# Products of zeros on TensorE in the later half of a first layer's head, and at its end

## The chip, the cores and the metric

One core of one Trainium2 chip runs the whole program. The metric is the device time of one execution in microseconds (us), from start to end; the kernel is launched once and computes everything.

## The reference

Two transformer layers on x of shape (2, 1024, 256) in float32. Layer 0 is causal attention with 16 heads of width 16 in 4 groups (each group shares its key and value head), with unit-length queries and keys, rotary tables, and then a feed-forward product on block-quantised operands. Layer 1 is causal attention with 16 heads and a mixture of eight experts. A layer norm follows each. Only the beginning of layer 0 matters here:

```python
q = (x @ Wq + bq)...; k = (x @ Wk + bk)...; v = (x @ Wv + bv)...
q_hat = q / (norm(q) + EPS); k_hat = k / (norm(k) + EPS)
q_r = apply_rope(q_hat * alpha * sqrt(hd)); k_r = apply_rope(k_hat)
scores = einsum(q_r, k_r) / sqrt(hd)    # causal, softmax, times v
```

## The kernel before

The program is written by hand: each engine has one list of instructions, run in order, and semaphores tie the lists together. PE is TensorE, DVE is VectorE, ACT is ScalarE, POOL is GpSimd, SP is the engine that issues the transfers.

The **head** (`head()`) makes the queries and keys of layer 0. Its work is cut into 12 units (`NU`), u = 0 to 11: four chunks m of 512 tokens by three tiles n of 128 rows (two of queries, one of keys). A unit goes through these steps, each on its engine:

- PE `projected(u)` (L649), four recorded pieces of a product in float32 into bank A.
- PE `begin(u)` (L667): one product of zeros, one row by 128 weights by 512 columns in bfloat16, that opens bank R + u % 2, after a wait for `s_sq`, that is until ACT has read what stood there two units before.
- DVE `turned(u)` (L799, two instructions), after `begin(u)`. One goes straight into the opened bank.
- PE `rotate(u)` (L673, two pieces), which adds the rotated half to that bank.
- ACT `keep(u)` (L750 copy, L754 square), the square goes on to PE `lengths(u)` (L684: 8 pieces of 4 or 8 columns, into bank N = 7).
- Once three units of a chunk have their lengths, DVE `factors(m, 0)` and `factors(m, 1)` (L838 to L855, some twenty small instructions on 80 columns) work out the inverse lengths, PE `factors(m)` turns them (L697), ACT copies them (L771).
- PE `spread_factors(u)` (L707, 60 rows by 512 columns), DVE `normalised(u)` (L808), ACT `keep_hi(u)` (L758), DVE `less_hi(u)` (L815), ACT `keep_mid(u)` (L762), POOL (L787): the unit is cut into three bfloat16 parts in `parts_mem`. POOL counts them in `s_parts`.

PE's list runs over u = 0 to 20 (`NU + LATER + 2` with `LATER` = 7): in round u it does `projected(u)` and `begin(u)` while u < 12, the spreading of unit u - 7 from round 7 on, the rotation of unit u - 1, the lengths of unit u - 2. `factors(m)` stands in rounds 7, 10, 13 and 16. Rounds 14 to 20 hold only spreading products, one transpose group, and in round 14 the value products of chunks 2 and 3 (L657, 32 pieces).

The last round is followed by `attention`. PE waits there for the stacked operands of the first item (`ops.there(pe, 0)`) and computes scores (L1200), ACT takes the exponential (L1285), PE multiplies by the values (L1217). The operands are stacked by SP: `stack(sp, 0)` waits until six units are in parts (`sp.wait_ge(s_parts[self.layer], TILES[self.layer] * 2 * (b + 1))`), then issues 20 transfers one after another (L944 to L956). `stack(sp, 1)` and ACT's exponentials from the second step on wait for all twelve.

`none` is one row of 512 zeros in bfloat16; `P` is 128.

Of the kernel before, what the change touches and what calls it, by code (L numbers as in the profile page):

```python
# [15 lines left out]
P = 128  # L16
# [7 lines left out]
NC = NT // CT  # L24
# [44 lines left out]
def build(nc, a, out):  # L69
    ctx = ExitStack()  # L70
    with ctx:
        def sb(name, shape, dt=F32):
            return ctx.enter_context(nc.sbuf_tensor(name, shape, dt))

        def sem(name):
            return ctx.enter_context(nc.semaphore(name))

        ps = ctx.enter_context(nc.psum_tensor("ps", [P, 8, 512], F32))
# [3 lines left out]
        none = sb("none", [1, CH], BF16)  # L82
# [124 lines left out]
        def on(engine):  # L207
            def keep(f):
                programs[engine].append(f)
                return f  # L210
            return keep
# [31 lines left out]
        def loaded(eng, group):  # L243
            eng.wait_ge(s_load[group], 16 * len(loads[group]))
# [109 lines left out]

        def chunks(eng, body):

            body(0, False, True)
            with eng.Fori(1, NC - 1) as c:  # L360
                body(c, True, True)
            body(NC - 1, True, False)
# [235 lines left out]
        def head():  # L598
# [3 lines left out]
            NU = NTL * NC  # L602
            s_w4, s_yn = loop_sem("s_w4"), loop_sem("s_yn")
            s_w4q, s_w4t, s_w4k = sem("s_w4q"), sem("s_w4t"), sem("s_w4k")
            s_a, s_a_read, s_rot, s_kept, s_sq = sem("s_a0"), sem("s_a_read"), sem("s_rot0"), sem("s_kept"), sem("s_sq0")
            s_n2, s_n2_read = sem("s_n2"), sem("s_n2_read")
# [5 lines left out]
            A, R, S, N = 0, 2, 4, 7  # L612
# [6 lines left out]
            def unit(u):  # L619
                return u // NTL, u % NTL  # L620
# [7 lines left out]
            def turned_factors(m):  # L628

                return ps[0:3 * NY, S + NTL * m % 3, 0:CH // 2].bitcast(BF16)  # L630
# [7 lines left out]
            @on("tensor")  # L638
            def _(pe):
                def room(m, n):  # L640

                    if AT[m, n] >= 2:
                        pe.wait_ge(s_a_read, AT[m, n] - 1)

                def projected(u):
                    m, n = unit(u)
                    room(m, n)
                    for kk in range(2):
                        last = nc.tensor.matmul(ps[:, A + AT[m, n] % 2, :], w0qkv[:, kk, n * P:(n + 1) * P],  # L649
                                                xT0[:, kk, m * CH:(m + 1) * CH], start=kk == 0, stop=kk == 1)  # L650
                    last.then_inc(s_a, 1)

                def values(m):
                    room(m, NTL)
                    for t in range(CT):
                        for kk in range(2):
                            last = nc.tensor.matmul(ps[:, A + AT[m, NTL] % 2, t * 64:(t + 1) * 64],  # L657
                                                    xT0[:, kk, m * CH + t * P:m * CH + (t + 1) * P],
                                                    w0qkv[:, kk, 3 * P:3 * P + 64], start=kk == 0, stop=kk == 1)
                    last.then_inc(s_a, 1)  # L660

                def begin(u):


                    if u >= 2:
                        pe.wait_ge(s_sq, u - 1)
                    nc.tensor.matmul(ps[:, R + u % 2, :], none[:, 0:P], none[:, :], start=True, stop=False  # L667
                                     ).then_inc(s_begun, 1)

                def rotate(u):  # L670

                    pe.wait_ge(s_a_read, AT[unit(u)] + 1)
                    nc.tensor.matmul(ps[:, R + u % 2, :], perm[:, :], u_sin[:, u % 2, :], start=False, stop=True  # L673
                                     ).then_inc(s_rot, 1)

                def lengths(u):
                    m, n = unit(u)
                    pe.wait_ge(s_sq, u + 1)
                    if n == 0 and m > 0:

                        pe.wait_ge(s_n2_read, m)
                    lo, w = (8 * n, 8) if n < 2 else (HEADS, NG)
                    for t in range(CT):
                        last = nc.tensor.matmul(ps[:, N, t * NY + lo:t * NY + lo + w],  # L684
                                                sq0[:, u % 8, t * P:(t + 1) * P],
                                                hsum[:, 0:8] if n < 2 else hsum[:, 8:12], start=True, stop=True)
                    last.then_inc(s_n2, 1)

                def factors(m):
                    pe.wait_ge(s_ysp, m + 1)  # L690

                    if m > 0:
                        pe.wait_ge(s_rest, NTL * m - 2)
                    else:
                        pe.wait_ge(s_w4k, 1)
                    for t in range(CT):
                        last = nc.tensor.transpose(turned_factors(m)[:, t * P:(t + 1) * P],  # L697
                                                   ysp[:, m % 2, t, :], identb[:, :])
                    last.then_inc(s_ynt, 1)

                def spread_factors(u):
                    m, n = unit(u)
                    pe.wait_ge(s_ynk, m + 1)

                    if u >= 3:
                        pe.wait_ge(s_rest, u - 2)
                    nc.tensor.matmul(ps[:, S + u % 3, :], spread[:, n, :], ynT[:, m % 2, :], start=True, stop=True  # L707
                                     ).then_inc(s_bc, 1)

                loaded(pe, "qkv")  # L710
                for u in range(NU + LATER + 2):
                    if u < NU:
                        if u % NTL == 0:
                            loaded(pe, f"x{u // NTL}")
                        projected(u)
                        begin(u)
                    if NU <= u < NU + 2:
                        lengths(u - 2)
                    if 0 <= u - LATER < NU:
                        if (u - LATER) % NTL == 0:  # L720
                            factors((u - LATER) // NTL)
                        spread_factors(u - LATER)
                    if 0 <= u - 1 < NU:
                        if u == 1:
                            loaded(pe, "rope")
                        rotate(u - 1)
                    if 2 <= u < NU:
                        if u == 2:
                            loaded(pe, "head")
                        lengths(u - 2)  # L730
                    if u < 2 * NTL and u % NTL == NTL - 1:
                        values(u // NTL)
                    if u == NU + 2:
                        values(2)
                        values(3)
                    if u == 3:
                        pe.wait_ge(s_w4q, 1)
                        pt = ps[:, S, 0:256].bitcast(BF16)
                        for kk in range(2):
                            for r in range(2):  # L740
                                last = nc.tensor.transpose(pt[:, kk * C + r * P:kk * C + (r + 1) * P],
                                                           w4a[:, r, kk * P:(kk + 1) * P], identb[:, :])
                        last.then_inc(s_w4t, 1)
                loaded(pe, "late")

            @on("scalar")
# [916 lines left out]
        def tail(first, gates_of, bank_free, outputs_there, layer=1):  # L1663
# [65 lines left out]
            def _(pe):  # L1729
# [73 lines left out]

                pe.wait_ge(s_exp_w, 16 * len(expert_weights["first"]))
                chunks(pe, body)

            @on("vector")
            def _(dve):
# [50 lines left out]

                gates_of.choose(dve, 0)  # L1860
                chunks(dve, body)

                for half in range(2):
# [144 lines left out]
```

## Time and profile before

| | us |
|---|---|
| median of 3 runs | 828.75 (826.79 to 828.79) |
| profiled execution, its own time | 832.21 |
| its span, first to last instruction | 830.5 |
| mean granted TensorE clock | 0.931 of full speed |

A granted clock of 1.00 is 2.4 GHz, one of 0.50 is 1.2 GHz. Rows of a timeline give start, duration, engine, line, operation, out<-in, shape and count, and in brackets how long the engine stood idle before and what released it. Busy time of PE is the time for which matmuls are recorded, with ends that are modelled. Times of rows are microseconds from the start of the span.

### The profile page before, as it was taken

The page shows a single profiled execution, that of the slowest core. Times are in us where ns is not written, and L with a number is a line of the kernel's source. Part 1 is how long each engine was busy: PE and PEld are TensorE (multiplying, and loading weights), DVE is VectorE, ACT ScalarE, POOL GpSimd, SP SyncE. Part 2 cuts the span into 40 slices and gives each one's busy share as a digit, 9 for nine tenths or more (in the row PEclk, how much of TensorE's full clock was granted, in tenths as well). Part 3 has the DMA queues.
Part 4 walks back from the last instruction along what each step waited for, and adds up shares of the span by engine and source line. Part 5 has one row for each costly group of instructions (what it writes and reads, how often), then busy time and mean ns, then how long its engine had stood idle before and what let it go on. Part 6 is the DMA issues. An engine that isn't in the chain of part 4 may idle for free.

```text
span 830.5 us, 10867 instructions
## 1 busy us (share of the span) xinstructions
PE 740.5 (89%) x3786; PEld 334.7 (40%) x3786; DVE 402.6 (48%) x988; ACT 400.1 (48%) x526; POOL 168.7 (20%) x187
## 2 busy tenths in 40 slices
PE   5989599999997669678599999999999999999995
PEld 2645222222323425324122222323448448448355
DVE  2776515333277779763233333245452752552524
ACT  1242588888784253433488888784120220221110
POOL 0012324442333122221324322331200200000000
PEclk9995599999999789688799999998999999999998
DMA  8300333332300000013335554570000000000000
GB/s 291 90 0 1 65 57 65 57 56 52 56 4 2 1 0 14 0 20 59 59 61 90 83 86 81 82 209 5 1 0 1 25 2 1 25 0 0 25 1 26
DMA packets 31603, 36.37 MB, mean 44 GB/s; under 512 B 7665, under 2 KB 19758, under 8 KB 31390
## 3 DMA queue, kind: packets, MB, share of 16 engines
q1 hardware_dynamic: 31541, 35.60, 21.1%
q8 instruction: 33, 0.54, 0.3%
q14 instruction: 29, 0.23, 0.1%
HBM read 12.74 MB, written 2.10 MB: 18 GB/s over the span
## 4 chain that ended last, share of the span: by engine, by line
PE 59%; DVE 13%; SPq 11%; ACT 8%; issue 5%; DMA 3%; POOL 1%; DVEq 0%; ACTq 0%; POOLq 0%
PE ps L1770 17%; PE ps L1217 10%; PE ps L1200 9%; PE ps L1794 8%; ACT probs L1285 6%; SPq L944 5%; SPq L951 4%; PE ps L1436 2%; PE ps L649 2%; DVE stats L285 2%; PE ps L673 2%; PE ps L684 1%; PE ps L1409 1%; PE ps L428 1%; PE ps L1780 1%
## 5 line engine op out<-in xcount | busy, mean ns | idle before, releaser
L1285 ACT ACTIVATE probs<-ps 128x1024 f32<-128x1024 f32 (+1 forms) x320 | 275.8, 966 | 63.0 <-PE ps L1200 62.1
L1200 PE MATMUL ps<-ops_mem 99*128 99x512 bf16 (+3 forms) x768 | 164.7, 336 | 14.9 <-issue 10.7
L1217 PE MATMUL ps<-probs,vstat 128*32 128x512 f32 (+3 forms) x1536 | 166.6, 506 | 9.3 <-DVE raw L1134 3.7
L1770 PE MATMUL ps<-ops_mem,parts_mem 128*128 128x512 f32 x320 | 147.4, 606 | 1.2 <-DVE probs L1822 1.2
L1301 POOL TENSOR_SCALAR_AFFINE_SELECT probs<-probs 128x512 f32<-128x512 f32 x128 | 88.0, 689 | 226.8 <-ACT probs L1285 226.4
L1200 PEld LDWEIGHTS ps<-ops_mem 99*128 99x128 bf16 x768 | 57.5, 99 | 167.7 <-ACT probs L1285 89.2
L1134 DVE COPY raw<-ps 128x512 f32<-128x512 f32 x32 | 22.1, 691 | 162.2 <-PE ps L1217 161.9
L1716 ACT ACTIVATE ops_mem<-ps 128x512 f32<-128x512 f32 x40 | 23.9, 597 | 143.1 <-PE ps L1770 143.1
L1770 PEld LDWEIGHTS ps<-ops_mem,parts_mem 128*128 128x128 f32 x320 | 58.9, 191 | 68.9 <-issue 66.2
L1794 PE MATMUL ps<-parts_mem,probs 128*128 128x256 f32 x320 | 70.5, 380 | 0.0
L1794 PEld LDWEIGHTS ps<-parts_mem,probs 128*128 128x128 f32 x320 | 60.3, 190 | 8.4 <-issue 0.5
L1217 PEld LDWEIGHTS ps<-probs,vstat 128*32 128x32 f32 x1536 | 31.5, 108 | 72.2 <-issue 52.5
L1817 DVE TENSOR_TENSOR probs<-ops_mem,ps 128x512 f32<-128x512 f32 x40 | 27.5, 687 | 63.8 <-ACT ops_mem L1716 63.1
L649 PE MATMUL ps<-yT,probs 128*128 128x512 f32 x48 | 27.3, 697 | 7.6 <-DMA yT<-in_xT 7.6
L1141 DVE STREAM_TRANSPOSE den<-raw 128x512 f32<-128x512 f32 x32 | 22.7, 709 | 22.1 <-DMA yT<-in_zeros 21.5
L1545 POOL TENSOR_TENSOR parts_mem<-probs,parts_mem 128x512 bf16<-128x512 f32 x16 | 18.4, 1156 | 68.8 <-ACT parts_mem L1502 68.8
L750 ACT COPY ops_mem<-ps 128x512 f32<-128x512 f32 x12 | 7.0, 586 | 49.4 <-PE ps L673 49.4
L1422 PE MATMUL ps<-ops_mem,w1qkv 128*128 128x512 f32 x64 | 30.4, 596 | 0.0
L787 POOL TENSOR_TENSOR parts_mem<-probs,parts_mem 128x512 bf16<-128x512 f32 x12 | 13.9, 1155 | 79.5 <-ACT parts_mem L762 79.4
L1146 DVE TENSOR_TENSOR yT<-raw,den 128x512 f32<-128x512 f32 x32 | 28.6, 893 | 1.1
L1822 DVE TENSOR_TENSOR probs<-probs,ps 128x512 f32<-128x512 f32 x32 | 22.0, 687 | 10.2 <-PE ps L1780 8.0
L278 DVE TENSOR_TENSOR ops_mem<-ps,xres 128x1024 f32<-128x1024 f32 x12 | 14.6, 1217 | 23.9 <-PE ps L1794 23.9
(176 smaller groups left out, 733.9 us busy)
## 6 DMA issues: line engine op xcount, KB each, us to landing
ops_mem<-parts_mem SPq DMA_DIRECT2D x288, 64.0 KB
yT<-in_xT SPq DMA_DIRECT2D x4, 512.0 KB, 7.5
xres<-in_x SPq DMA_DIRECT2D x1, 2048.0 KB, 14.8
ops_mem<-parts_mem SPq DMA_DIRECT2D x48, 32.0 KB
out<-ops_mem SPq DMA_DIRECT2D x3, 512.0 KB, 2.9
rope<-in_rope SPq DMA_DIRECT2D x1, 1024.0 KB, 6.8
parts_mem<-in_wg SPq DMA_DIRECT2D x2, 512.0 KB, 4.9
parts_mem<-in_wu SPq DMA_DIRECT2D x2, 512.0 KB, 6.9
```

The source lines that it names most:

```text
L649: last = nc.tensor.matmul(ps[:, A + AT[m, n] % 2, :], w0qkv[:, kk, n * P:(n + 1) * P], xT0[:, kk, m * CH:(m + 1) * CH], start=kk == 0, sto ...
L944: sp.dma_start(qT[n * HD:n * HD + HD, buf, j::2, :], tq[32 * g + HD * j:32 * g + HD * j + HD, Q_PARTS[n], :, toks]).then_inc(s, 16)
L951: sp.dma_start(kT[n * HD:n * HD + HD, buf, j::2, :], tk[32 * g + HD * j:32 * g + HD * j + HD, K_PARTS[n], :, toks]).then_inc(s, 16)
L1146: nc.vector.tensor_tensor(yT[:, i, c * CH:(c + 1) * CH], raw[:, :], den[:, :], ALU.mult).then_inc(s_y, 1)
L1200: last = nc.tensor.matmul(ps[:, bank, o:o + CH - lo], kT[0:KDIM, buf, h if kh == GH else 0, kt * P:(kt + 1) * P], qT[0:KDIM, buf, h, c * C ...
L1217: last = nc.tensor.matmul(ps[32 * h:32 * h + 32, av_bank(i, c), lo:CH], vstat[:, i % 2, kt, h if kh == GH else 0, :], probs[:, s % PRING, ...
L1285: nc.scalar.activation(o, banks, ACT.Exp, scale=score_scale).then_inc(s_exp, 1)
L1301: nc.gpsimd.affine_select(out=block_, in_=block_, compare_op=ALU.is_ge, fill=0.0, base=0, pattern=[[0, GH], [1, P]], channel_multiplier=-1 ...
L1422: last = nc.tensor.matmul(ps[:, A + n % 2, :], w1qkv[:, kk, n * P:(n + 1) * P], xT1[:, kk, :], start=kk == 0, stop=kk == 1)
L1770: last = nc.tensor.matmul(ps[:, 4 + 2 * (e % 2) + m, :], w, xT[:, kk, :], start=kk == 0, stop=kk == 1)
L1794: last = nc.tensor.matmul(ps[:, t // 2, (t % 2) * C:(t % 2) * C + C], hT[:, e, t * P:(t + 1) * P], w, start=e == 0, stop=e == NE - 1)
L1817: o = vec.tensor_tensor(hT[:, e, :], silu[:, e % 2, :], u, ALU.mult)
```

## The change

A helper `nothing(bank, times)` issues `times` products of zeros (one row, 128 weights, 512 columns, bfloat16) into a bank, each closed in itself. It is used in three places of PE's list of the head:

- in `begin(u)` after the wait and ahead of the opening product: two for u = 8 to 11, none before; 8 in all
- in rounds 14 to 20, ahead of `factors` and `spread_factors`: a wait until ACT has squared all twelve units, then three; 21 in all
- after the last round: a wait until DVE has read the last lengths, then eight into bank 7

That makes 37 products. No other engine's list changes, and nothing reads what they write.

```diff
+        def nothing(bank, times):
+
+            for _ in range(times):
+                nc.tensor.matmul(ps[:, bank, :], none[:, 0:P], none[:, :], start=True, stop=True)
...
                     if u >= 2:
                         pe.wait_ge(s_sq, u - 1)
+                    nothing(R + u % 2, 2 if u >= 8 else 0)
                     nc.tensor.matmul(ps[:, R + u % 2, :], none[:, 0:P], none[:, :], start=True, stop=False
                                      ).then_inc(s_begun, 1)
...
                     if NU <= u < NU + 2:
                         lengths(u - 2)
+                    if u >= NU + 2:
+
+                        pe.wait_ge(s_sq, NU)
+                        nothing(R + u % 2, 3)
                     if 0 <= u - LATER < NU:
...
                         last.then_inc(s_w4t, 1)
+
+                pe.wait_ge(s_n2_read, NC)
+                nothing(N, 8)
                 loaded(pe, "late")
```

## Rows read from the trace of the kernel before

**Rows 1.** The page: granted clock of TensorE in 40 slices, in tenths.

```profile
PEclk9995599999999789688799999998999999999998
```

**Rows 2.** Stretches of 48 to 120 us: busy by engine, granted clock, DMA.

```profile
48.00:60.00 12.00, 10.50 (x41) 5.15 (x41) 11.26 (x26) 5.06 (x9) 2.31 (x2) 1.00 0.00 0
...
61.00:74.00 13.00, 13.00 (x31) 6.62 (x30) 10.48 (x25) 3.44 (x7) 2.31 (x2) 0.50 0.00 1
...
86.50:95.00 8.50, 2.71 (x8) 0.67 (x7) 6.50 (x20) 3.33 (x6) 2.44 (x3) 0.50 0.50 86
99.00:104.50 5.50, 5.45 (x20) 1.59 (x20) 0.23 (x1) 4.26 (x5) 1.94 (x3) 0.50 0.36 65
104.50:120.00 15.50, 15.36 (x115) 4.26 (x112) 0.82 (x2) 12.90 (x15) 3.63 (x6) 1.00 0.34 59
```

**Rows 3.** Chain that ended last, 38 to 99 us: start, duration, piece.

```profile
38.67 0.32 PE ps L667
38.99 1.06 PE ps L673 x2
40.05 0.79 PE ps L684 x8
40.84 1.82 PE ps L649 x4
...
61.66 3.62 PE ps L649 x4
...
66.35 2.00 PE ps L673 x2
68.35 3.21 PE ps L684 x16
...
82.22 0.78 SPq L944
...
94.50 2.88 DMA ops_mem<-in_ones
97.37 1.62 issue
```

**Rows 4.** Timeline of TensorE around 57 us.

```profile
56.89 0.41 PE L697 MATMUL ps<-identb,probs 128*60 128x128 bf16 x4
58.80 0.39 PE L707 MATMUL ps<-probs 60*128 60x512 bf16 x1 [1.50 <-ACT probs L771]
```

**Rows 5.** Timeline of VectorE, 61 to 80 us.

```profile
61.82 0.24 DVE L838 TENSOR_SCALAR small<-ps 128x80 f32<-128x80 f32 x1 [1.31 <-PE ps L684]
...
70.70 1.10 DVE L855 TENSOR_TENSOR probs<-small,probs 128x80 bf16<-128x80 f32 x1
...
79.03 0.70 DVE L808 TENSOR_TENSOR ps<-ps,ops_mem 128x512 f32<-128x512 f32 x1 [5.60 <-PE ps L707]
```

**Rows 6.** Chain: four products of 99 rows by 512 columns, at either clock.

```profile
111.14 0.97 PE ps L1200 x4
...
562.94 1.82 PE ps L1200 x4
```

**Rows 7.** Timeline of TensorE and POOL, 91 to 100 us.

```profile
91.98 1.03 PE L707 MATMUL ps<-probs 60*128 60x512 bf16 x2 [2.75 <-ACT probs L771]
94.06 0.58 PE L707 MATMUL ps<-probs 60*128 60x512 bf16 x1 [1.04 <-DVE probs L815]
97.32 2.35 POOL L787 TENSOR_TENSOR parts_mem<-probs,parts_mem 128x512 bf16<-128x512 f32 x2 [0.33 <-ACT parts_mem L762]
```

**Rows 8.** Stretches of the second layer in which the clock changed or stayed.

```profile
305.00:309.00 4.00, 3.36 (x5) 1.17 (x5) 1.90 (x3) 3.12 (x7) 0.00 (x0) 0.50 0.00 0
309.00:311.00 2.00, 0.83 (x6) 0.10 (x4) 0.69 (x1) 2.00 (x5) 1.07 (x1) 0.91 0.00 0
...
572.00:575.60 3.60, 3.60 (x40) 2.53 (x40) 0.19 (x1) 1.01 (x2) 1.27 (x2) 1.00 0.00 0
575.60:579.00 3.40, 3.40 (x19) 1.39 (x8) 2.62 (x6) 1.51 (x2) 0.00 (x0) 0.50 0.00 0
```

## The prediction

> **What bounds the kernel now.** I read the page first: its strip of the granted clock shows three places where it leaves full speed; the first, slices 4 and 5, lies in the head [rows 1]. Then stretches around it: up to 60 us the clock is 1.00, from 61 to 104.5 us it is 0.50, after that 1.00 again [rows 2]. A cold clock costs only where TensorE sets the end, so the chain comes next. From 61.66 to 79 us it runs almost wholly through TensorE: four pieces of L649 take 3.62 us where the same four took 1.82 at the full clock, two of L673 take 2.00 for 1.06, sixteen of L684 take 3.21 where eight took 0.79 [rows 3]. At 82.22 us the chain goes over to SP, which now issues the first stack, and it stays with SP until 94.50; a transfer and 1.62 us until its semaphore is seen end it at 99.00, where the scores begin [rows 3]. From 86.5 us on TensorE does hardly anything: 2.71 us in 8.5 [rows 2], and nothing between the last product of the head at 94.06 [rows 7] and the scores. What starts the first stack is the sixth unit of POOL. ACT makes its middle part only behind the high part of the seventh in its list, and so it hangs on the spreading in round 13 of TensorE, which released L808 at 79.03 [rows 5].
>
> **What the clock did.** Before it fell, TensorE had short work: four transposes at 56.89 us, 1.50 us idle, one product of 60 rows at 58.80 [rows 4]. After that it ran busy for 13 us at 0.50 and did not rise [rows 2]. So the question has two parts: is the fall at 60 us avoided, and is the clock up when attention begins?
>
> **Rounds 8 to 11 (8 products).** A product of zeros alone has one price in sequence, L667 at 0.32 us [rows 3]; several behind each other are not in the trace. The nearest are four products of 99 rows by 512 columns: 0.97 us at the full clock, 1.82 at half, so 0.24 and 0.455 each [rows 6]. I take these, and 0.32 warm as the upper bound. Rounds 8, 9 and 10 add six, 1.46 us, but the first four lie under VectorE, on whose list the chain runs there. The transposes of 56.89 come at 58.35, ACT copies them a half microsecond later than now, so L707 comes at 59.3 instead of 58.80: +0.5 on the path. The hole ahead of it shrinks from 1.50 [rows 4] to about 0.6 us, and nearly 1 us of L649 and 0.7 us of zeros move into the stretch before 60. Round 11 adds two on the path: 0.5 us warm, 0.9 cold.
>
> **What it gives if the clock holds.** The cold surcharge on the chain from 60 to 79 us: L649 1.80; L673 twice, 0.94 each; L684 3.21 against 2 x 0.79, 1.63 [rows 3]. That is 5.3, and the smaller pieces in between, in the same ratio, make it about 8. Not all of it comes back, since VectorE is late next: its work on the factors of chunk 2 starts at 61.82 and its last piece ends at 71.80, 10.0 us without a hole worth naming, and none of it depends on the clock [rows 5]. It would start at about 61.7 (0.6 us sooner, since the eight lengths ahead of it were cold for the most part, and 0.5 later by the shift) and end at 71.7. The transposes (0.4, as at 56.89 [rows 4]), ACT's copy (0.6) and the spreading (0.4, as at 58.80 [rows 4]) then give L808 at 73.1 instead of 79.03 [rows 5]: 6 us. But rounds 12 and 13 get no zeros, and TensorE waits there for those factors, so I expect the clock to fall near 67 to 71 us. If it falls at 67, the lengths and the rotation of units 10 and 11 are cold and up to 2 us of the 6.0 go. I take 5.0 for the first stack, with 4.0 and 6.0 as ends.
>
> **Rounds 14 to 20 and the end (29 products).** The waits added are on the last square, which round 13's lengths have waited for already, and on VectorE's reading of the last lengths, with which it begins the factors of chunk 3, three rounds before the end; they hold nobody. The first three delay L657, which has slack under VectorE. Those of rounds 16, 17 and 18 stand ahead of the last transposes and spreadings: nine products, 4.1 us cold. The spreadings of rounds 16 and 18 wait for ACT and VectorE now, 2.75 and 1.04 us of idle before them [rows 7], which hides most; about 1 to 2 us remain on the last two units, cold, and none warm. After the last spreading (94.06 + 0.58) come fourteen, 3.4 us warm and 6.4 cold, in the 4.4 us until the scores at 99.00 [rows 3, 7]. Warm they fit; cold they overhang by 2 us, with the late spreading by 3 to 4. All products together are 9 us warm and 17 cold; the cover is the idle time of 86.5 to 99 us.
>
> **Attention warm instead of cold.** From 99.0 to 104.5 us the clock is 0.50 [rows 2]. ACT, with its exponentials, is busy for 4.26 of these 5.50 us [rows 2], and its work does not depend on the clock, so a full clock can give back at most 1.24 us; I take 1.1, zero if the clock is still down.
>
> **Do these products keep the clock?** No row shows one-row products alone. Two stretches speak. At 305 to 309 us TensorE ran four pieces of L1436 of 128 rows, behind one product of one row, at 0.50 and the clock rose (0.91 as the mean of the next 2 us) [rows 8]. From 61 to 74 us it was as busy, with products of one and of 60 rows and pieces of 8 columns among the others, and it did not rise [rows 2]. From 572 to 575.6 TensorE is recorded busy throughout, 40 short pieces, and the clock falls behind it [rows 8]. The products here have 512 columns, like the good case, but one row, unlike it. I hold it slightly likelier that they count.
>
> The Trainium skill (TensorE: Matmul & The Clock Gate, "Part 1: The HAM clock gate") says that the clock is set by how busy the PE has been; by that rule alone any product helps, zeros or one row, and the time would be that of the forecast, 823.5; without it the slower rival has 832 to 834. The trace disagrees in part: the stretch of 572 to 575.6 us was busy in the record and the clock fell all the same [rows 8].
>
> **The sum.** Against the profiled execution (832.2 us, span 830.5): stack and all parts 5.0 sooner, attention warm 1.1, an overhang of the zeros of 0.5 (spreading at about 90, zeros until 93.5 to 94.5, the stack there at 94.0): -5.6, so 826.6. The profiled execution is 3.5 above the median of the runs. I put the same difference on the median and take 0.3 off it, since other executions may lose their clock somewhat later than this one: 828.75 - 5.3 = 823.5. Own range 820.5 (6.0 + 1.1 + other small waits) to 826.2.
>
> **Rivals.**
> - *The products don't count for the clock* (slower, 0.22). It falls at 60 us as now, or at once after. Then rounds 8 to 11 cost 0.5 + 0.9, and fourteen cold products stand between the last spreading and the scores: spreading at 96 to 98, plus 6.4, scores at 103 to 104 instead of 99.0, and attention just as cold. +3.5 to +5, 832 to 834. For it: the cold busy stretch at 61 to 74 us. Against it: the shift of L649 fills the hole at 57 us whatever zeros count. It decides from where the clock is below full when the fourteen are reached: 6.4 us don't fit into 4.4.
> - *Gain and overhang cancel* (0.27). The clock holds at 60 by the shift alone, SP starts 4 to 6 us sooner, but it is cold in the tail, so the scores start only 0 to 3 us sooner. Or it falls in some executions and not in others. 826.3 to 830.5, likeliest 827.
> - *SP was not the bound, or nothing happens* is part of the same case: if the first stack started sooner and its 20 transfers met others, they would lose time; but there is no other traffic between 61 and 79 us (DMA share 0.00 [rows 2]), so I give that next to nothing.
>
> **How the numbers follow.** Forecast 0.51, cancelling 0.27, slower rival 0.22. A difference of 0.3%, 2.5 us, is about what a measurement of this kernel can tell from none. Of the forecast all but 0.02 is faster by more than that; of the cancelling case 0.04 is faster and 0.22 within. Of the slower rival 0.03 stays within. That gives faster 0.53, within 0.28, slower 0.19. The range goes from 820.5 to 832.0: it leaves out some 0.05 below and most of the rival's upper half, 0.13.
>
> **What would show it.** Right: a granted clock of 1.00 past 60.5 us; L649 of round 11 in 1.8 us; the first SP issue (L944) near 76 to 78 instead of 82.22; the first scores at 93 to 95 and the clock 1.00 from them on. The rows of the zeros in rounds 14 to 20 tell the price: 0.24 or 0.455 each. Wrong: a clock of 0.50 at 61 us, SP at 83 or later; a clock of 0.50 over the last fourteen products, with the scores released by TensorE's own list and not by the transfer. A gain at the scores that attention gives back would be a wait of ACT on all twelve parts (POOL ends them at 99.67 now, 97.32 + 2.35 [rows 7]): if the last spreadings are late by 2 us, ACT's second step waits for POOL.

## The result, and the profile after

The changed kernel takes 832.0 us (median of 20 runs, 829.27 to 836.17), the kernel before 829.0 (20 runs, 825.73 to 834.08): a ratio of 1.0035, with an interval of 1.0020 to 1.0051, so 2.9 us slower (1.7 to 4.2). I had forecast 823.5.

The profile after has a span of 830.8 us. Its stretches, in the columns of [rows 2]:

```profile
60.00:61.00 1.00, 1.00 (x9) 0.76 (x7) 0.84 (x2) 0.40 (x1) 0.00 (x0) 1.00 0.00 0
61.00:74.00 13.00, 11.44 (x45) 6.78 (x44) 10.02 (x25) 6.24 (x12) 3.34 (x3) 0.72 0.01 1
...
86.50:95.00 8.50, 7.83 (x20) 1.96 (x19) 5.22 (x9) 4.97 (x9) 3.46 (x3) 0.50 0.32 60
95.00:99.00 4.00, 4.00 (x11) 1.32 (x9) 0.71 (x2) 1.04 (x2) 2.26 (x2) 0.50 0.03 6
99.00:104.50 5.50, 5.45 (x22) 1.63 (x20) 0.04 (x1) 3.91 (x5) 1.04 (x2) 0.50 0.45 77
```

The clock is 1.00 past 60 us, as forecast, and falls in the stretch behind it (0.72 as a mean of 61 to 74, 0.50 before [rows 2]). But from 86.5 to 99 us TensorE is busy for 11.83 of 12.5 us, some 9.6 of them with the new products, and the granted clock stays at 0.50; in attention's first 5.5 us as well.

The chain that ended last (start, duration, piece; L360 is the product of zeros; L654, L662, L679, L713 and L1213 are L649, L657, L673, L707 and L1200 of before) shows where it decides:

```profile
61.36 1.82 PE ps L654 x4
...
68.61 2.02 PE ps L679 x2
...
77.42 7.02 PE ps L662 x32
...
92.91 0.54 PE ps L713
93.44 6.08 PE ps L360 x14
99.53 3.10 PE ps L1213 x8
```

L654 takes 1.82 us, as forecast, where the profile of before had 3.62 [rows 3]. Then the last fourteen products take 6.08 us, 0.434 each, and the scores follow straight behind them. Before, the chain came to the scores from SP and a transfer [rows 3]; here it comes from TensorE's own list. SP's first issue is sooner and the scores are not:

```profile
78.73 1.44 SPq L957 DMA_DIRECT2D ops_mem<-parts_mem  x2
```

78.73 us against 82.22 [rows 3], but scores at 99.53 against 99.00.

### The profile page after: what moved, and what is told of

Its sections match the earlier page's. It is cut to its first block, busy times and chain, and to the rows that moved or that the text cites. A ratio compares the mean times of both kernels' runs of the same rounds, so it can differ in the third digit from the quotient of the medians.

```text
span 830.8 us, 10941 instructions
## 1 busy us (share of the span) xinstructions
PE 748.9 (90%) x3823; PEld 335.9 (40%) x3823; DVE 402.6 (48%) x988; ACT 400.8 (48%) x526; POOL 168.2 (20%) x187
## 4 chain that ended last, share of the span: by engine, by line
PE 67%; DVE 11%; ACT 8%; SPq 7%; issue 4%; DMA 2%; POOL 1%; DVEq 0%; ACTq 0%; POOLq 0%
PE ps L1783 16%; PE ps L1230 11%; PE ps L1213 10%; PE ps L1807 8%; ACT probs L1298 6%; SPq L964 3%; PE ps L654 3%; SPq L957 3%; PE ps L399 2%; PE ps L1449 2%; PE ps L360 2%; PE ps L679 2%; PE ps L1435 1%; PE ps L1422 1%; PE ps L662 1%
## 5 line engine op out<-in xcount | busy, mean ns | idle before, releaser
L1213 PE MATMUL ps<-ops_mem 99*128 99x512 bf16 (+3 forms) x768 | 164.9, 336 | 11.5 <-issue 5.5
L1213 PEld LDWEIGHTS ps<-ops_mem 99*128 99x128 bf16 x768 | 57.5, 99 | 164.4 <-ACT probs L1298 91.2
L1154 DVE STREAM_TRANSPOSE den<-raw 128x512 f32<-128x512 f32 x32 | 22.7, 709 | 20.7 <-DMA yT<-in_zeros 20.1
L654 PE MATMUL ps<-yT,probs 128*128 128x512 f32 x48 | 25.2, 651 | 7.9 <-DMA yT<-in_xT 7.9
```

The lines of the kernel that those rows point to most:

```text
L1213: last = nc.tensor.matmul(ps[:, bank, o:o + CH - lo], kT[0:KDIM, buf, h if kh == GH else 0, kt * P:(kt + 1) * P], qT[0:KDIM, buf, h, c * C ...
```

## The experiments

Theory A: one-row products do nothing for the clock; whatever is gained at the first stack is not theirs, and the fourteen cold ones stand ahead of the scores. Theory B: the tail is hidden and the gain is lost elsewhere. A1 and A2 are two reasons for A: too few rows, or zero as a value.

**Rounds 8 to 11 alone** (`e1_rounds8_11`). Left out of the change:

```diff
-                    if u >= NU + 2:
-                        pe.wait_ge(s_sq, NU)
-                        nothing(R + u % 2, 3)
...
-                pe.wait_ge(s_n2_read, NC)
-                nothing(N, 8)
```

> Only the eight products of rounds 8 to 11 are kept; those of rounds 14 to 20 and the final eight are gone. Theory A (the one-row products do nothing for the clock; the gain at the first stack comes from the shift of other work, the loss from the cold products of the tail): SP starts its first stack near 77 us as with the whole change, TensorE's list is free of the tail, the scores start at 94 to 95 instead of 99.5, the clock is 0.50 there. 825 to 828, 2 to 5 us faster than before. Theory B (the gain at the first stack is lost in SP, DMA or ACT anyway, the tail is innocent): scores still at 99, 829 to 832, no gain.

829.5 us (12 runs), ratio 0.9997 (0.9973 to 1.0020): the loss of the whole change is gone, so it sits in the tail. The gain of 2 to 5 us that I expected is not there, though. In this profile the clock fell near 60.4 us in spite of the six products that stand ahead of that time, and L654 was cold (timeline of TensorE):

```profile
60.01 1.36 PE L690 MATMUL ps<-hsum,yT 128*128 128x4 f32 x8
61.23 3.76 PE L654 MATMUL ps<-yT,probs 128*128 128x512 f32 x4
64.92 1.03 PE L360 MATMUL ps<-none 1*128 1x512 bf16 x2
```

**The tail alone** (`e2_tail_only`: `nothing(R + u % 2, 2 if u >= 8 else 0)` left out).

> Only the 29 products of rounds 14 to 20 and of the end are kept. Theory A: clock falls near 60 us as before, SP near 82, the last spreading some 1.5 to 2.5 us later and 14 products of 0.43 us at half clock behind it, so the scores start at 102 to 103.5 instead of 99.0: 832 to 835, slower than the whole change. Theory B: the products of the tail lie under the wait for the transfer: 828.5 to 830.

834.26 us (10 runs), ratio 1.0053 (1.0021 to 1.0085). SP began at 81.05, the fourteen took 6.15 us from 95.69, and the scores started at 101.77, all near what theory A expects.

**128 rows in place of one** (`e3_rows128`). The tile is an unused part of `raw`, filled once by POOL, for which PE waits once ahead of the first round; the 37 products stay where they are.

```diff
+        wide = raw[0:128, 0:CH // 2].bitcast(BF16)
...
-                nc.tensor.matmul(ps[:, bank, :], none[:, 0:P], none[:, :], start=True, stop=True)
+                nc.tensor.matmul(ps[:, bank, :], wide[:, 0:P], wide[:, :], start=True, stop=True)
...
+                nc.gpsimd.memset(wide[:, :], 0.0).then_inc(s_wide, 1)
```

> The whole change, but each of the 37 products reads 128 rows of zeros (a tile filled once at the start) instead of one row; columns, number and place are the same. Theory A1 (the number of rows is what the one-row products lack): the clock is back at 1.00 before the last fourteen are through (they stand at 93 to 99 us), these take 3.4 to 5 us in place of 6.1, and attention starts at full clock: scores near 95 to 97, 824 to 828. Theory A2 (it is the zero values, or the clock needs something else than rows): the fourteen at 0.50 throughout, 6.1 us, 831 to 833 as with the change.

829.11 us (12 runs), ratio 0.9998 (0.9977 to 1.0019): the loss of the change is gone, but the 824 to 828 that A1 expected is not reached. Timeline of TensorE and, below it, the chain of this run (L362 is the product, L705 the transposes):

```profile
84.72 1.46 PE L362 MATMUL ps<-raw 128*128 128x512 bf16 x3
86.11 0.41 PE L705 MATMUL ps<-identb,probs 128*60 128x128 bf16 x4
...
89.83 3.13 PE ps L362 x14
92.96 1.21 issue
94.17 0.60 PE ps L1217 x2
```

The first products of the tail are still at half clock (1.46 us for three), the transposes behind them at the full one. The fourteen take 3.13 us, 0.224 each, and TensorE waits again behind them. The chain names no releaser for that wait; that it is the transfer follows from SP's first issue at 77.25, 16.9 us ahead of the scores, as in the kernel before (table below). Its stretches:

```profile
86.50:95.00 8.50, 6.51 (x28) 2.41 (x28) 4.48 (x7) 5.09 (x10) 5.77 (x5) 1.00 0.24 47
95.00:99.00 4.00, 3.08 (x17) 0.84 (x15) 0.23 (x1) 4.00 (x5) 1.27 (x2) 0.67 0.40 69
99.00:104.50 5.50, 5.50 (x31) 1.44 (x28) 0.00 (x0) 2.36 (x4) 1.27 (x2) 0.62 0.50 83
```

The clock is up from 86.5 us on, as A1 says, but it falls again near 96.4 us, within attention's first microseconds. Short waits for ACT between the products there are not enough to explain it: `e7_warm128` and `e12_tail128` below have the same waits and keep the full clock. So the attention at full clock that I had counted (1.1 us) came only in part, even here.

**One row of ones** (`e4_ones_1row`: the same with `raw[0:1, ...]` and 1.0) and **32 rows of zeros** (`e8_rows32`: `raw[0:32, ...]`).

> The whole change, but the 37 products read one row of ones instead of one row of zeros. Theory A1 (rows): no difference from the change, the clock 0.50 through the last fourteen products, 831 to 833. Theory A2 (values: zeros toggle nothing, ones do): the clock rises in the tail, 824 to 828.

832.39 us (12 runs, timed together with those of 128 rows, which took 829.11), ratio 1.0023 (1.0004 to 1.0041).

> The whole change with 32 rows of zeros in place of one. If one row is treated like a whole group of 32, or the count of rows enters in proportion, 32 rows are still too few: clock 0.50 through the last fourteen, 831 to 833, as with the change. If some rows are enough: clock up in the tail as with 128 rows, 828 to 830.

831.53 us, ratio 1.0031 (1.0006 to 1.0056). The fourteen, of ones and of 32 rows:

```profile
98.05 6.15 PE L362 MATMUL ps<-raw 1*128 1x512 bf16 x14
```

```profile
92.47 6.15 PE L362 MATMUL ps<-raw 32*128 32x512 bf16 x14
```

Both at half clock from the first to the last. Between 1 and 32 rows there is no difference, between zeros and ones of one row neither; with 128 rows of zeros the clock was up. A1 holds, A2 falls. That it is chance where the clock stands is not likely: in all six profiles with few-row products in the tail (the change twice, `e2_tail_only`, `e4_ones_1row`, `e8_rows32`, `e6_no_eight`) it stayed at 0.50 from 86.5 to 99 us, in all three with 128 rows it came up by 87.5 us. Numbers of rows between 32 and 128 were not tried, nor values that change from column to column. Nor did every dense run with 128 rows bring the clock up: the 32 value products of the change (L662, 128 rows by 64 columns in float32) ran for 7.02 us without a gap, and it stayed at 0.50.

**Without the final eight** (`e6_no_eight`: `nothing(N, 8)` and its wait left out).

> The change without the final eight products; those of rounds 8 to 11 and 14 to 20 stay, one row each. Theory A (cold products of the tail overhang the transfer): the last products end 3.5 us sooner and the scores start when the transfer is in or 3.5 us sooner: 829 to 830.5, about 2 us faster than the change. Theory B (the tail was hidden): no difference from the change, 832.

830.15 us, ratio 0.9993 (0.9973 to 1.0013): the loss is gone with these eight alone. Eight by 0.434 us is 3.5 us. In this profile the six that are left still run without a gap into the scores (101.00 us, 17.3 us behind SP), so at most some 0.6 us of the overhang stays.

**Before and the change once more** (`e5_before_again`, `e9_before_third`, `e10_change_again`), one profile each.

> The kernel before, unchanged, for another profile of it. Theory L (where the clock falls in the head differs from execution to execution, and the profile the prediction read was one of the dear ones): the fall comes at another time than 60.2 us, the last L649 group may be warm, SP starts before 82.2, the span is 826 to 829. Theory F (the fall is fixed by the program): fall at 60.2 us again, SP at 82.2 again, span 830.5.

> The kernel before, a third profile. Theory L (the place where the clock falls in the head differs between executions): another start of the first scores than 99.00 and 97.42 us, between 96 and 100. Theory F (always the same): 99.0 again.

> The changed kernel, a second profile. Whatever the phase, theory A expects the clock at 0.50 through the last fourteen products (6.1 us) and the scores released by TensorE's own list, 2 to 4 us after the transfers are in; the start of the scores at 98 to 103. Theory B (the overhang of the first profile was chance): scores released by the transfer.

The group that followed the fall, in the second and the third profile of before, and SP's first issue in each:

```profile
62.10 3.69 PE L649 MATMUL ps<-yT,probs 128*128 128x512 f32 x4
...
80.91 1.44 SPq L944 DMA_DIRECT2D ops_mem<-parts_mem  x2
```

```profile
60.55 3.49 PE L649 MATMUL ps<-yT,probs 128*128 128x512 f32 x4
...
79.00 1.44 SPq L944 DMA_DIRECT2D ops_mem<-parts_mem  x2
```

Theory L: the same program loses 0 to 3 us more or less in the head. In all three profiles of before the clock is down over much of this stretch, but for how long differs (up again for some 3 us from about 65 and 64 us in the second and third, as the pieces behind that group show), and the scores start at 99.00, 97.42 and 95.93. The profile that the prediction was read from is the dearest of the three: 832.21 us, against 831.18 and 829.42, and 3.2 us above the median of 20 runs. In `e10_change_again` SP began at 77.41, the fourteen took 6.15 us from 92.05, the scores started at 98.13: the overhang of the first profile was not chance.

**With more products of 128 rows** (`e7_warm128`: 128 rows, three in rounds 12 and 13 as well, twelve at the end), **in rounds 8 to 13 only** (`e11_mid128`), **in the tail only** (`e12_tail128`). The edit is shown against the change; all three have the 128-row tile of `e3_rows128` as well, and `e12_tail128` has beside that only the products of `begin(u)` left out.

```diff
-                    if u >= NU + 2:
+                    if u >= NU:                  # e7; e11: if NU <= u < NU + 2
-                        pe.wait_ge(s_sq, NU)
+                        pe.wait_ge(s_sq, min(NU, u - 1))
                         nothing(R + u % 2, 3)
...
-                nothing(N, 8)
+                nothing(N, 12)                   # e7; not in e11
```

> Products of 128 rows of zeros in place of one row, three of them in rounds 12 and 13 as well, and twelve instead of eight at the end. Theory A1 (rows matter, and the hole of rounds 12 and 13 is what let the clock fall at 67 us with 128 rows): clock 1.00 from 60 us to the scores, SP at 76 to 77, scores at 93 to 95, 824 to 827. Rival (products ahead of the last units delay them as much as the clock gives back): 828 to 830.

830.16 us, ratio 0.9996 (0.9977 to 1.0016), not the 824 to 827 of A1. The clock did not hold from 60 us to the scores: it was 0.50 from 74 to 86.5 us.

> Products of 128 rows of zeros in rounds 8 to 11 (two each) and 12 and 13 (three each), none from round 14 on. Theory A1 (the clock is held until the spreading of round 13 and the tail is empty): SP at 76 to 78.5, scores at 94 to 95.5, attention cold at its start: 826 to 828.5. Rival (the 14 products add 3 us warm to the path of the first stack, which is what a held clock returns against a typical execution of before): 829 to 831, no gain.

828.07 us, ratio 0.9988 (0.9960 to 1.0017).

> Products of 128 rows of zeros only in rounds 14 to 20 (three each) and eight at the end; nothing in rounds 8 to 11. Theory A1: SP's first stack as before (80 to 82 us), the fourteen last products at full clock (3.2 us) and hidden under the transfer, scores as before at 97 to 99, attention at full clock from its start, 1 us to gain: 828 to 829.5. Rival (the clock falls again at the start of attention, whose products stand apart there, so nothing is left of it): 829.5 to 831.

828.81 us, ratio 1.0007 (0.9982 to 1.0031). The clock was 1.00 from 86.5 to 120 us, so the rival's reason, that it falls when attention starts, is not what happened.

None of the three can be told from before, though scores started at 96.02, 93.87 and 95.18. In `e7_warm128` and `e12_tail128` the chain no longer ran through TensorE behind the scores but through SP's second stack and the transfer of zeros that VectorE waits for (timeline of VectorE, `e7_warm128`):

```profile
119.71 0.71 DVE L1158 STREAM_TRANSPOSE den<-raw 128x512 f32<-128x512 f32 x1 [14.10 <-DMA yT<-in_zeros]
```

That stack starts when POOL has all twelve units, which the scores' start does not move. Yet nothing is lost by it in these two profiles: the last column below is no longer than that of before.

**The profiles side by side.** From SP's first issue to the first scores, and from there to the end of the span, in us, worked out from each timeline:

| kernel | products in rounds 8-11 | SP | scores | between | scores to end |
|---|---|---|---|---|---|
| before, 3 profiles | none | 82.22, 80.91, 79.00 | 99.00, 97.42, 95.93 | 16.8, 16.5, 16.9 | 731.5, 732.1, 731.8 |
| e1 | 1 row | 82.79 | 99.19 | 16.4 | 733.0 |
| change, 2 profiles | 1 row | 78.73, 77.41 | 99.46, 98.13 | 20.7, 20.7 | 731.3, 731.6 |
| e2, tail only | none | 81.05 | 101.77 | 20.7 | 734.4 |
| e4, ones | 1 row | 83.41 | 104.14 | 20.7 | 730.3 |
| e8 | 32 rows | 77.83 | 98.55 | 20.7 | 731.2 |
| e6, without the eight | 1 row | 83.69 | 101.00 | 17.3 | 730.4 |
| e3, e7 | 128 rows | 77.25, 78.69 | 94.17, 96.02 | 16.9, 17.3 | 731.8, 730.5 |
| e11 | 128 rows | 77.33 | 93.87 | 16.5 | 731.7 |
| e12, tail, 128 rows | none | 78.21 | 95.18 | 17.0 | 731.4 |

(The chain puts the change's first scores at 99.53, its timeline at 99.46.) Three things stand in it. Every profile with the whole tail at half clock has 20.7 us between, all others 16.4 to 17.3: an overhang of 4.0 us, whatever SP's start. SP's start with few-row products in rounds 8 to 11 (e1, e4, e6, e8 and the change twice) is 80.6 on average, without any (before three times, e2, e12) 80.3, with 128 rows 77.8. But the six with few rows lie anywhere from 77.4 to 83.7, so a difference of a microsecond or two would not show. Last, the scores start over a range of 10 us, while what follows them differs by 4 and does not go with the kind of kernel: what an execution gains or loses by its first scores, it mostly keeps to the end.

## Why the prediction was wrong

- **The step that failed is "Do these products keep the clock?"** I held it slightly likelier that they count, from products of 512 columns in the good case of [rows 8], and gave the rival in which they don't 0.22. That rival is what happened in the tail: fourteen products at 0.434 us, no rise over 6.1 us without a gap, scores released by TensorE's own list. Its mark was in [rows 2]: 13 busy microseconds at 0.50, with products of few rows among them.
- **The overhang** was a term of 0.5 us in the sum and measured 4.0. The prices behind it were right: 6.08 us for fourteen where I had 6.4 cold, 3.13 where I had 3.4 warm. The Trainium skill (TensorE: Matmul & The Clock Gate, "Back-to-back issue gap") gives formulas for the gap from one single product to the next, by which 512 columns take an estimated 0.427 and 0.216 us each. The trace agrees, with 0.434 and 0.224 measured. I had even written 3 to 4 us for this case, and then taken the other.
- **The first stack, 5.0 us sooner.** In the profile after it is 3.5 us sooner than in the one of before, by the steps forecast: L654 in 1.82 us, the clock falling near 67 us, SP 78.73. But that compares one execution with another. Over the profiles at hand, no gain by products of few rows in rounds 8 to 11 can be seen (SP at 80.6 against 80.3), and e1, with these alone, was timed at 0.9997 of before: in e1, e4 and e6 the clock fell between 60.4 and 61 us all the same, and in e1 the two products of round 11 then took 1.03 us cold. The shift of 0.5 us that I had put at 58.80 [rows 4] can't be told: that spreading starts at 59.12 in the change and 58.73 in e1, and at 58.80, 58.39 and 58.46 before. "The shift of L649 fills the hole at 57 us whatever zeros count" was right for some executions only.
- **The base of the sum.** I read one profile, the dearest of three now at hand, 3.5 us above the median that I forecast from, and put its whole cold surcharge down as there to be gained. The others had lost 1.6 and 3.1 us less by the scores. I had allowed 0.3 for that. The Trainium skill (TensorE: Matmul & The Clock Gate, "Part 1: The HAM clock gate") says that where the clock turns varies between runs of one kernel. The three profiles of before agree, with first scores from 95.93 to 99.00. I should have had a term for this.
- **Attention at full clock, 1.1 us.** Not measured in the change, where the clock was 0.50. In e3, where it was up when the scores began, it fell again (0.67, 0.62); in e7 and e12 it stayed at 1.00 until 120 us. To have it up at the start is not to keep it. What it gives where it is kept is small: from the first scores to the end e7 and e12 took 730.5 and 731.4 us, against a mean of 731.8 before, in one profile each.
- **The sum as it came out**: nothing that could be shown from the stack, +4.0 of overhang, of which the timed runs show +2.9 (1.7 to 4.2) in the change, +4.4 us (1.7 to 7.1) with the tail alone and none without the final eight. This accounts for the result. Why the change comes out nearer to 3 than to 4 is not settled; the interval holds both.
- **What stays open**: with 128 rows the scores start 1.4 to 3.6 us sooner than in the mean of before (97.45), yet no timed difference is clear. The profiles compare unlike executions. Those with 128 rows (827.69, 828.20, 827.28 and 828.34 us) lie 0.5 to 2.0 us below the medians of their kernels, the first of before 3.2 us above its own, and what follows the scores is no longer than before in all four, so nothing was lost there. So a good part of these microseconds is which execution was profiled, and the timed ratios, 0.9988 to 1.0007, are what counts. Whether 128 rows bring a microsecond is not settled.

## What to carry to other kernels

Work put in to keep a clock up must be shown to do so before its place is tuned: look whether the granted clock stands or rises behind a dense run of exactly that product, and if the trace has none, measure one. Filler behind the last useful product is free only if its price at the lower clock fits the wait that covers it; here 6.1 us stood against 2.1 (from the last spreading at 93.44 to 95.5, when the transfers of a stack begun at 78.73 would have released the scores, 16.8 us later, by the table). And where the clock's turns differ between executions, read two or three profiles of the kernel before putting down what one of them lost as a gain, and look how far each profiled execution lies from the median.

## What the runs showed of the hardware

- Fourteen products of one row (zeros or ones) or of 32 rows by 512 columns ran at a granted clock of 0.50 for 6.1 us without a gap, and it did not rise; the same with 128 rows of zeros, with the clock up since about 86 us, took 3.13 us. That zeros are no hindrance, this last run shows too. The Trainium skill (TensorE: Matmul & The Clock Gate, "Part 1: The HAM clock gate") says that the clock is set by how busy the PE has been. The trace disagrees in part: the PE was recorded busy for 6.1 us without a gap, and for 11.83 of the 12.5 us from 86.5 us on, and stayed at 0.50.
- Thirty-two pieces of 128 rows by 64 columns in float32 ran for 7.02 us without a gap at 0.50 too, and the clock did not rise behind them in the change.
- Of the kernel before, three executions of the same program started its first scores at 99.00, 97.42 and 95.93 us. Of the 3.1 us between them at most 0.4 stood already at 58 us, ahead of the fall (the spreading at 58.80, 58.39 and 58.46); the rest came in the head behind it, where the clock was up for some 3 us in the second and third and not in the first.
